# Two reorderings in the late attention steps of a four-layer conditioned sequence model, on one NeuronCore

## The chip, the cores and the metric

One NeuronCore of one Trainium2 chip runs the whole program. The metric is device time in microseconds (us) of one execution. The engines are TensorE (PE in the profile, its weight loads PEld), VectorE (DVE), ScalarE (ACT), GpSimd (POOL) and SyncE (SP, which only issues DMAs here). Each engine runs its own list of instructions in order, and waits on counting semaphores that other engines raise.

## The reference, cut to what matters

Four layers are applied to x of 64 sequences x 64 tokens x 256 features. The change touches the attention half of the second one (16 heads of 16 features, `split` makes the heads, `t` is the condition of a sequence):

```
def _rmsnorm(x):
    return x * jax.lax.rsqrt(jnp.mean(x * x, axis=-1, keepdims=True) + EPS)
...
def _ada_rmsnorm(x, t, gamma_w, beta_w):
    gamma = (t @ gamma_w.T)[:, None, :]
    beta = (t @ beta_w.T)[:, None, :]
    return gamma * _rmsnorm(x) + beta
...
q = split(x @ W_q.T)
k = split(x @ W_k.T)
v = split(x @ W_v.T)
attn = jax.nn.softmax(scale * jnp.einsum('bnqd,bnkd->bnqk', q, k), axis=-1)
o = jnp.einsum('bnqk,bnkd->bnqd', attn, v)
o = o.transpose(0, 2, 1, 3).reshape(b, l, dm)
return o @ W_o.T
...
x = x + a_alpha * _attention(_ada_rmsnorm(x, t, attn_gamma_w, attn_beta_w), W_q, W_k, W_v, W_o)
```

The first layer before it is a quantised gated MLP, the second half of the second layer is a SwiGLU MLP, the third is an adapter with weights made for each sequence, and the fourth is a layer norm with a conditional shift. All are computed in fp32 accuracy, with each matmul's operands split into a high and a low part (three products in place of one).

## The kernel before, in words

The kernel is written by hand for each engine. The program runs through four stages, one after the other and overlapped at their edges: the first layer up to about 224 us of the trace, attention up to about 383 us, the SwiGLU MLP up to about 690 us, adapter and norm to the end.

Attention works on 16 tiles of 256 tokens (4 sequences). It is a software pipeline of 17 steps, t = 0 to 16: the function `attention_body(s)` of each engine writes what that engine does in step t, for tiles of different age. `s.live(n)` means that tile t - n exists. Steps up to 8 are written out one by one ("peeled"), steps 9 to 14 are a hardware loop of two steps a turn, steps 15 and 16 are written out again. `plain(s)` is true for steps 9 to 16, `before_plain(s)` for 8 to 16. In a plain step t:

- TensorE, in this order: `scores` of tile t-2 (L1215), `transposes(s, 0)` of tile t-3 (L1237), `output` of tile t-4 (L1281), `transposes(s, 1)` of tile t-3, then `keys` and `queries` of tile t-1 (both L1156, 12 matmuls each, keys first), `weighted_values` of tile t-3 (L1254), `values` of tile t-1 (L1191).
- GpSimd: the attention input of tile t is made in four operations on 128x512 elements, in `attention_input`: part 0 multiplies x by its row scale (L182), part 1 multiplies by gamma (L186) and adds beta (L188), part 2 subtracts the high part to give the low part (L191). Between parts 1 and 2 it adds the attention output to x (`residual`, L1056). Behind part 2 it normalises the softmax of tile t-2 in two halves of 128x1024, `normalise(s, 0)` and `normalise(s, 1)` (both L1047). Part 0 for the next step's tile is issued at the end of the step, from step 8 on.
- ScalarE: `take_values` (L1465 to L1469), `take_transposed(s, 0)` (L1448), `exponentials(s, 0)` (L1440), `take_transposed(s, 1)`, `attention_input_high` of tile t (L198), which rounds the input to its high part, `exponentials(s, 1)`, `take_keys` of tile t-1 (L1476, two instructions), `take_queries` (L1485), `output_high` (L1491).
- VectorE: `maxima` of the two halves (L1643, L1647) with `scaled_output` between them (L1678), `sums` of the two halves (L1655, L1658), `output_low` (L1664).

What ties the engines together near the change: `transposes(s, 1)` in step t waits for `normalise(s, 1)` of step t-1 (semaphore `norm_done`). `take_keys` waits for the key matmuls (`k_ready`). `attention_input_high` waits for part 1 (`h_done`), and part 2 on GpSimd waits for `attention_input_high` (`h_hi_done`). `exponentials(s, 1)` stands ahead of `sums(s, 1)` on VectorE, whose reciprocal (L1658) `normalise(s, 1)` needs. Part 0 waits for part 2 of the tile before it, because both use the one buffer `mlp_in`. Tiles called `mlp_in`, `mlp_in_hi`, `mlp_in_lo`, `att_in_hi` and `att_in_lo` in L182 to L198 are that attention input.

After step 15 GpSimd makes the MLP's first input (L812, L816, L819), with the last normalisations and residuals between its parts, and TensorE goes over from attention to the MLP.

Of the kernel before, what the change touches and what calls it, by code (L numbers as in the profile page):

```python
# [92 lines left out]
def wait(eng, sem, count):  # L93

    if not isinstance(count, int) or count > 0:
        eng.wait_ge(sem, count)
# [72 lines left out]
def attention_input(nc, pool, core, s, part):  # L169

    x, cond, stat, h, S = core["x"], core["cond"], core["stat"], core["att_in"], core["att_sems"]
    t = s.at(0)
    hi, lo = (parts[s.slot(0, 2)] for parts in core["att_parts"])
    hb = h[:].rearrange("p h (b l) -> p h b l", b=GB1)

    def of_batches(v):
        return cond[:, v, :, bass.ds(t * GB1, GB1)].unsqueeze(3).to_broadcast([P, DH, GB1, L])

    if part == 0:
        pool.wait_ge(core["stat_loaded"], 16 * s.turn(0, 2))  # L180
        wait(pool, S["h_ready"], t)
        nc.gpsimd.tensor_tensor(h[:], x[:, :, bass.ds(t * GT1, GT1)], stat[:, bass.ds(t * GT1, GT1)].unsqueeze(1).to_broadcast([P, DH, GT1]),  # L182
                                ALU.mult).then_inc(S["xn_done"], 1)
    elif part == 1:
        pool.wait_ge(S["xn_done"], 2 * t + 1)
        nc.gpsimd.tensor_tensor(hb, hb, of_batches(GAMMA1), ALU.mult).then_inc(S["xn_done"], 1)  # L186
        pool.wait_ge(S["xn_done"], 2 * t + 2)
        nc.gpsimd.tensor_tensor(hb, hb, of_batches(BETA1), ALU.add).then_inc(S["h_done"], 1)  # L188
    else:
        pool.wait_ge(S["h_hi_done"], t + 1)  # L190
        nc.gpsimd.tensor_tensor(lo, h[:], hi.bitcast(FP32), ALU.subtract).then_inc(S["h_ready"], 1)  # L191


def attention_input_high(nc, act, core, t, k):

    S = core["att_sems"]
    act.wait_ge(S["h_done"], t + 1)
    nc.scalar.activation(core["att_parts"][0][k], core["att_in"][:], ACT.Copy).then_inc(S["h_hi_done"], 1)  # L198
# [633 lines left out]
def layers(nc, io, core, bank, keep, early, adapter_w, base_w, slot_loaded, out):  # L832
# [19 lines left out]
    with ExitStack() as c:  # L852
# [79 lines left out]
        def pair_of(ap, two):  # L932

            return ap[:, 2 * two:2 * two + 2, :].rearrange("p u k -> p (u k)")
# [5 lines left out]
        def plain(s):  # L940

            return not isinstance(s.t, int) or s.t > PEELED

        def before_plain(s):

            return not isinstance(s.t, int) or s.t >= PEELED
# [11 lines left out]
        def groups(ap):  # L958
            return ap.rearrange("p (a k) -> p a k", k=L)
# [81 lines left out]
        def _(pool):  # L1041
            def normalise(s, two):
                if s.live(2):
                    u = s.at(2) * PAIRS + two
                    pool.wait_ge(A["rec_done"], u + 1)
                    pu = groups(pair_of(p, two))
                    nc.gpsimd.tensor_tensor(pu, pu, rec[:, two, :].unsqueeze(2).to_broadcast([P, 16, L]),  # L1047
                                            ALU.mult).then_inc(A["norm_done"], 1)

            def residual(s):  # L1050
                if s.live(4):
                    t = s.at(4)
                    xt = x[:, :, bass.ds(t * GTA, GTA)]
                    pool.wait_ge(A["ya_done"], t + 1)
                    hold(pool, A["passed"])
                    nc.gpsimd.tensor_tensor(xt, xt, ya1[:], ALU.add).then_inc(A["x_done"], 1)  # L1056

            def attention_body(s):
                following = Step(s.t + 1, s.k + 1, NA, s.turns)
                if s.live(0):  # L1060
                    if not plain(s):
                        attention_input(nc, pool, core, s, 0)
                    attention_input(nc, pool, core, s, 1)
                    if s.first_tile(4):
                        first["row_scales"](pool, e35)
                    if plain(s):
                        residual(s)
                    if s.first_tile(3):
                        normalise(s, 0)
                    wait(pool, A["v_ready"], s.at(1) if s.live(2) else 0)  # L1070
                    attention_input(nc, pool, core, s, 2)
                    if not plain(s):
                        residual(s)
                if not s.first_tile(3):
                    normalise(s, 0)
                normalise(s, 1)
                if before_plain(s) and following.live(0):
                    attention_input(nc, pool, core, following, 0)

            def generator_base():  # L1080
                pool.wait_ge(A["base_loaded"], 32)
                nc.gpsimd.tensor_scalar(delta_bias, delta_bias, 0.1, None, ALU.mult).then_inc(A["base_done"], 1)
                pool.wait_ge(A["base_done"], 1)
                nc.gpsimd.tensor_tensor(base, base, delta_bias, ALU.add).then_inc(A["base_done"], 1)
# [350 lines left out]
        def _(act):  # L1435
            def exponentials(s, two):
                if s.live(2):
                    u = s.at(2) * PAIRS + two
                    act.wait_ge(A["sub_done"], u + 1)
                    nc.scalar.activation(pair_of(p, two), pair_of(p, two), ACT.Exp, scale=SCALE).then_inc(A["exp_done"], 1)  # L1440
# [20 lines left out]
            def take_values(s):  # L1461
                if s.live(2):
                    act.wait_ge(A["v_ready"], s.at(2) + 1)
                    wait(act, A["pv_ready"], s.at(3) if s.live(4) else 0)
                    nc.scalar.activation(value_slots(s, 0, 0), value_sums(s, 0, 0), ACT.Copy)  # L1465
                    nc.scalar.activation(value_slots(s, 0, 1), value_sums(s, 0, 1), ACT.Copy).then_inc(A["v_low_done"], 1)
                    if not vector_takes_values(s):
                        nc.scalar.activation(value_slots(s, 1, 0), value_sums(s, 1, 0), ACT.Copy)
                        nc.scalar.activation(value_slots(s, 1, 1), value_sums(s, 1, 1), ACT.Copy).then_inc(A["v_high_done"], 1)  # L1469

            def take_keys(s):
                if s.live(1):
                    act.wait_ge(A["k_ready"], s.at(1) + 1)
                    wait(act, A["s_ready"], UNITS * (s.at(1) - 1) if s.live(3) else 0)
                    for parity in range(2):
                        ins = nc.scalar.activation(ks[:, s.slot(1, 2)].rearrange("p c b e k -> p (c b) e k")[:, :, parity, :],  # L1476
                                                   bank[1].rearrange("p (a k) -> p a k", k=L), ACT.Copy,
                                                   scale=vecs[:, V_EVEN + parity:V_EVEN + parity + 1])
                    ins.then_inc(A["k_done"], 1)

            def take_queries(s):
                if s.live(1):
                    act.wait_ge(A["q_ready"], s.at(1) + 1)
                    ps = bank[5] if s.first_tile(1) else bank[2]
                    nc.scalar.activation(qs[:, s.slot(1, 2)], ps[:, :].rearrange("p (c t) -> p c t", c=2), ACT.Copy).then_inc(A["q_done"], 1)  # L1485
# [14 lines left out]
            def attention_body(s):  # L1500
                take_values(s)
                if s.first_tile(3):
                    first["square_rows"](act, e34)
                    first["take_x"](act, e35)
                if s.first_tile(3):
                    take_keys(s)
                take_transposed(s, 0)
                exponentials(s, 0)
                first_two = s.first_tile(3) or s.first_tile(4)
                take_transposed(s, 1)  # L1510
                if first_two:
                    exponentials(s, 1)
                if s.first_tile(3):
                    take_queries(s)
                if s.live(0):
                    wait(act, A["v_ready"], s.at(1) if s.live(2) else 0)
                    attention_input_high(nc, act, core, s.at(0), s.slot(0, 2))
                if not first_two:
                    exponentials(s, 1)
                if not s.first_tile(3):  # L1520
                    take_keys(s)
                    take_queries(s)
                output_high(s)
                if s.first_tile(4):
                    first["take_lines"](act, e37)
                rstd(s)
                square(s)
# [658 lines left out]
```

## Time and profile before

| | |
|---|---|
| median of 3 runs | 741.57 us (741.37 to 742.21) |
| the profiled execution | 741.11 us, of which the span of the trace is 739.3 us |
| PE busy, whole span | 721.8 us (98%) |
| PEld busy | 586.4 us (79%) |
| DVE busy | 514.7 us (70%) |
| POOL busy | 410.6 us (56%) |
| ACT busy | 359.3 us (49%) |
| granted TensorE clock, all 40 slices | 9 tenths or more |

A busy share is an average over the four stages. What the change is worth has to be read in the attention stage, from which instruction waits for which. PE's busy time there is modelled (matmuls overlap), so a PE row that looks unbroken can still hide a wait of a few tenths of a us.

### The profile page before, as it was taken

How to read it: one execution, taken by the hardware profiler on the slowest of the kernel's cores; microseconds unless marked ns; L12 is line 12 of the kernel's file. 1: busy time of each engine (PE TensorE's matmuls, PEld its weight loads, DVE VectorE, ACT ScalarE, POOL GpSimd, SP SyncE). 2: the span in 40 equal slices, each digit the busy share in tenths (PEclk: the TensorE clock that was granted, in tenths of full speed). 3: DMA queues.
4: the chain of work that ended last, by engine and by line, in shares of the span. 5: the costliest groups of instructions: out<-in, count | busy, mean ns of one | idle time of the engine just before them, and what ended most of it. 6: DMA issues, size and time to landing. Idle time of an engine off the chain costs nothing.

```text
span 739.3 us, 18704 instructions
## 1 busy us (share of the span) xinstructions
PE 721.8 (98%) x6700; PEld 586.4 (79%) x6700; DVE 514.7 (70%) x808; ACT 359.3 (49%) x722; POOL 410.6 (56%) x408
## 2 busy tenths in 40 slices
PE   9999999999999899999999999999999999999996
PEld 8888888888888788888888777777777767778884
DVE  4977777777789989888995465656655566453466
ACT  4534444344447677888874333333333332322585
POOL 5645655554678888999997624224242423320244
PEclk9999999999999999999999999999999999999999
DMA  8854544445432000000004255577667777759943
GB/s 301 258 111 99 108 121 101 100 111 121 110 73 63 22 28 17 17 1 0 1 4 134 104 173 175 177 220 216 191 190 251 212 215 231 238 160 390 386 178 142
DMA packets 81339, 106.25 MB, mean 144 GB/s; under 512 B 39904, under 2 KB 53376, under 8 KB 81152
## 3 DMA queue, kind: packets, MB, share of 16 engines
q1 hardware_dynamic: 79840, 103.34, 46.7%
q10 hardware_dynamic: 1440, 2.11, 1.1%
q8 instruction: 39, 0.64, 0.4%
q14 instruction: 20, 0.16, 0.1%
HBM read 75.77 MB, written 21.27 MB: 131 GB/s over the span
## 4 chain that ended last, share of the span: by engine, by line
PE 75%; POOL 16%; issue 5%; DVE 3%; ACT 1%; DMA 0%; POOLq 0%; DVEq 0%; SPq 0%; ACTq 0%
PE banks L446 24%; PE banks L1317 22%; PE banks L1347 12%; POOL p_sb L1047 5%; PE banks L1369 4%; PE banks L530 4%; POOL mlp_in L182 2%; PE banks L1979 2%; PE banks L1949 2%; POOL mlp_in L186 2%; POOL x_sb L1056 2%; POOL att_in_lo L191 1%; PE banks L1971 1%; POOL mlp_in L188 1%; PE banks L548 1%
## 5 line engine op out<-in xcount | busy, mean ns | idle before, releaser
L629 ACT ACTIVATE gelu<-banks,rstd 128x512 f32<-128x512 f32 x64 | 44.0, 688 | 115.8 <-PE banks L446 114.1
L1699 DVE TENSOR_TENSOR g<-banks,silu 128x512 f32<-128x512 f32 x64 | 44.2, 690 | 77.6 <-PE banks L1317 44.9
L1703 DVE TENSOR_TENSOR g_lo<-g,g_hi 128x512 fp32r<-128x512 f32 x64 | 55.7, 870 | 47.6 <-ACT g_hi L1539 47.6
L1539 ACT ACTIVATE g_hi<-g 128x512 fp32r<-128x512 f32 x64 | 40.4, 631 | 96.0 <-DVE g L1699 95.0
L1533 ACT ACTIVATE silu<-banks 128x512 f32<-128x512 f32 x64 | 38.2, 597 | 97.4 <-PE banks L1317 97.4
L446 PE MATMUL banks<-up_hi,xs_hi 128*128 128x512 f32 x254 | 81.1, 400 | 0.0
L446 PE MATMUL banks<-up_hi,xs_lo 128*128 128x512 f32 x256 | 79.2, 391 | 0.0
L1317 PE MATMUL banks<-mlp_in_hi,w_hi 128*128 128x512 f32 x252 | 78.8, 394 | 0.0
L446 PE MATMUL banks<-up_lo,xs_hi 128*128 128x512 f32 x256 | 78.8, 390 | 0.0
L1317 PE MATMUL banks<-mlp_in_lo,w_hi 128*128 128x512 f32 x252 | 78.0, 390 | 0.0
L1317 PE MATMUL banks<-mlp_in_hi,w_lo 128*128 128x512 f32 x252 | 77.8, 390 | 0.0
L745 DVE SCALAR_TENSOR_TENSOR h<-banks,rstd,gelu 128x512 f32<-128x512 f32 x64 | 47.8, 747 | 37.0 <-ACT gelu L629 37.0
L822 POOL TENSOR_TENSOR mlp_in_lo<-mlp_in,mlp_in_hi 128x1024 fp32r<-128x1024 f32 x8 | 19.9, 2490 | 80.7 <-ACT mlp_in_hi L829 80.7
L1047 POOL TENSOR_TENSOR p_sb<-p_sb,rec 128x1024 f32<-128x1024 f32 x32 | 60.4, 1906 | 5.2 <-DVE rec L1658 5.2
L446 PEld LDWEIGHTS banks<-up_hi,xs_lo 128*128 128x128 f32 x256 | 48.1, 188 | 10.4
L446 PEld LDWEIGHTS banks<-up_lo,xs_hi 128*128 128x128 f32 x256 | 48.1, 188 | 10.2
L1317 PEld LDWEIGHTS banks<-mlp_in_lo,w_hi 128*128 128x128 f32 x252 | 47.3, 188 | 10.7
L1317 PEld LDWEIGHTS banks<-mlp_in_hi,w_hi 128*128 128x128 f32 x252 | 47.2, 188 | 10.8
L1317 PEld LDWEIGHTS banks<-mlp_in_hi,w_lo 128*128 128x128 f32 x252 | 47.3, 188 | 10.2
L1347 PE MATMUL banks<-g_hi,w_hi 128*128 128x512 f32 x128 | 52.6, 411 | 0.7 <-DVE g_lo L1703 0.7
L446 PEld LDWEIGHTS banks<-up_hi,xs_hi 128*128 128x128 f32 x254 | 45.4, 188 | 8.3 <-issue 0.2
L1347 PE MATMUL banks<-g_hi,w_lo 128*128 128x512 f32 x128 | 50.6, 395 | 0.0
(230 smaller groups left out, 1736.2 us busy)
## 6 DMA issues: line engine op xcount, KB each, us to landing
gen_hyper<-in_gen_t SPq DMA_DIRECT2D x32, 512.0 KB, 4.4
gen_made<-base_w SPq DMA_DIRECT2D x64, 256.0 KB, 4.4
adapter_w<-gen_made SPq DMA_DIRECT2D x64, 256.0 KB, 4.4
tokens<-in_x_tok SPq DMA_DIRECT2D x32, 128.0 KB, 2.3
w_stage<-in_w_t SPq DMA_DIRECT2D x32, 128.0 KB, 2.6
tokens_again<-in_x_tok SPq DMA_DIRECT2D x32, 128.0 KB, 2.2
weight_slot<-adapter_w SPq DMA_DIRECT2D x4, 1024.0 KB, 8.8
x_sb<-in_x_t SPq DMA_DIRECT2D x7, 512.0 KB, 6.3
```

The costliest lines, as they stand in the source:

```text
L446: last = nc.tensor.matmul(up_bank(s, j, part)[:, :], (xs_hi, xs_lo)[a][:, k, d, :], up[b][:, d, at:at + 512], start=start and d == 0, stop ...
L530: last = nc.tensor.matmul(y_ps, qt[:, s.slot(2, 2), f, :], downq[:, f, :], start=f == 0, stop=f == FC - 1)
L629: nc.scalar.activation(gelu[:, j, :], up_bank(s, j, 1)[:, :], ACT.Gelu, scale=rstd0[:, bass.ds(s.at(0), 1)]).then_inc(Z["gelu_done"], 1)
L745: nc.vector.scalar_tensor_tensor(out=h[:, k, j * 512:(j + 1) * 512], in0=up_bank(s, j, 0)[:, :], scalar=rstd0[:, bass.ds(t, 1)], in1=gelu[ ...
L1047: nc.gpsimd.tensor_tensor(pu, pu, rec[:, two, :].unsqueeze(2).to_broadcast([P, 16, L]), ALU.mult).then_inc(A["norm_done"], 1)
L1317: last = nc.tensor.matmul(chunk_bank(s, f, i)[:, :], w1[a][:, at:at + P], hs[b][k][:, d, :], start=n == d == 0, stop=n == 2 and d == DH - 1)
L1347: last = nc.tensor.matmul(bank[5 + m][:, :], w1[a][:, at:at + P], gs[b][:, f % 2, :], start=f == n == 0, stop=f == FC - 1 and n == 2)
L1369: last = nc.tensor.matmul(ps[B * half:B * (half + 1), :], scaled[rows, :], hyper[rows, k, half, :], start=True, stop=True)
L1533: nc.scalar.activation(silu[:, f % 2, :], chunk_bank(s, f, 0)[:, :], ACT.Silu).then_inc(S["silu_done"], 1)
L1539: nc.scalar.activation(gs[0][:, f % 2, :], g[:, f % 2, :], ACT.Copy).then_inc(S["g_hi_done"], 1)
L1699: nc.vector.tensor_tensor(g[:, f % 2, :], chunk_bank(s, f, 1)[:, :], silu[:, f % 2, :], ALU.mult).then_inc(S["g_done"], 1)
L1703: nc.vector.tensor_tensor(gs[1][:, f % 2, :], g[:, f % 2, :], gs[0][:, f % 2, :].bitcast(FP32), ALU.subtract).then_inc(S["g_ready"], 1)
```

## The change

Two edits, each a change of order and nothing else. No instruction is added or removed, and no operand changes.

```diff
--- before.py
+++ after.py
@@ -1073,9 +1073,9 @@
                         residual(s)
                 if not s.first_tile(3):
                     normalise(s, 0)
-                normalise(s, 1)
                 if before_plain(s) and following.live(0):
                     attention_input(nc, pool, core, following, 0)
+                normalise(s, 1)
 
             def generator_base():
                 pool.wait_ge(A["base_loaded"], 32)
@@ -1512,13 +1512,16 @@
                     exponentials(s, 1)
                 if s.first_tile(3):
                     take_queries(s)
+                if plain(s):
+                    take_keys(s)
                 if s.live(0):
                     wait(act, A["v_ready"], s.at(1) if s.live(2) else 0)
                     attention_input_high(nc, act, core, s.at(0), s.slot(0, 2))
                 if not first_two:
                     exponentials(s, 1)
+                if not plain(s) and not s.first_tile(3):
+                    take_keys(s)
                 if not s.first_tile(3):
-                    take_keys(s)
                     take_queries(s)
                 output_high(s)
                 if s.first_tile(4):
```

GpSimd, end of step 8, the first of seven steps (8 to 14) in which this order changes. `mlp_in<-x_sb,stat` is part 0 of the next tile's input, `p_sb<-p_sb,rec` a half of the normalisation.

```order
 L191 TENSOR_TENSOR mlp_in_lo<-mlp_in,mlp_in_hi 128x512
 L1056 TENSOR_TENSOR x_sb<-x_sb,y_alpha 128x2x256
-L1047 TENSOR_TENSOR p_sb<-p_sb,rec 128x1024 x2
-L182 TENSOR_TENSOR mlp_in<-x_sb,stat 128x512
+L1047 TENSOR_TENSOR p_sb<-p_sb,rec 128x1024
+L182 TENSOR_TENSOR mlp_in<-x_sb,stat 128x512
+L1047 TENSOR_TENSOR p_sb<-p_sb,rec 128x1024
```

Part 0 of the next input now stands ahead of the second half of the normalisation, which comes later by that one operation.

ScalarE, step 15; steps 9 to 14 change in the same way, and step 16, which has no `att_in_hi`, has the keys ahead of the exponential. `k_sb` are the keys, `att_in_hi` the high part of the input, `p_sb<-p_sb` the exponential of the second half.

```order
 L1440 ACTIVATE p_sb<-p_sb 128x1024
 L1448 ACTIVATE pt_sb<-banks 128x1024
+L1476 ACTIVATE k_sb<-banks,vecs 128x8x64 x2
 L198 ACTIVATE att_in_hi<-mlp_in 128x512
 L1440 ACTIVATE p_sb<-p_sb 128x1024
-L1476 ACTIVATE k_sb<-banks,vecs 128x8x64 x2
 L1485 ACTIVATE q_sb<-banks 128x512
 L1491 ACTIVATE ot_hi<-banks 128x512
```

The two copies of the keys now stand ahead of the input's high part and of the second exponential. The orders of TensorE, VectorE and SyncE are the same before and after.

## Rows read from the trace of the kernel before

**Rows 1.** The page: the chain that ended last, shares of the span.
```profile
PE 75%; POOL 16%; issue 5%; DVE 3%; ACT 1%; DMA 0%; POOLq 0%; DVEq 0%; SPq 0%; ACTq 0%
```

**Rows 2.** Chain of waits, 318 to 362 us: its shares by line.
```profile
by line: POOL p_sb L1047 31.7%; issue 27.7%; POOL mlp_in L182 14.3%; POOL mlp_in L186 9.5%; POOL x_sb L1056 7.2%; POOL att_in_lo L191 3.4%; POOL mlp_in_lo L191 3.2%; POOLq L86 0.9%; POOL mlp_in L188 0.8%; POOLq L182 0.7%; POOLq L186 0.6%; P
```

**Rows 3.** Busy time (and records) per engine, first of seven steps, and all.
```profile
297.61:307.58 9.97, 9.44 (x206) 8.49 (x205) 8.03 (x9) 7.83 (x14) 9.57 (x9) 1.00 0.10 31
...
sum 69.49, PE 67.72 PEld 61.66 DVE 61.12 ACT 56.37 POOL 67.01; mean PE 9.67 PEld 8.81 DVE 8.73 ACT 8.05 POOL 9.57
```

**Rows 4.** Timeline, GpSimd, 347 to 359 us: start, duration, line, operation.
```profile
347.41 3.77 POOL L1047 TENSOR_TENSOR p_sb<-p_sb,rec 128x1024 f32<-128x1024 f32 x2
351.14 1.30 POOL L182 TENSOR_TENSOR mlp_in<-x_sb,stat 128x512 f32 x1
352.63 1.05 POOL L186 TENSOR_TENSOR mlp_in<-mlp_in,cond_vectors 128x512 f32<-128x512 f32 x1 [0.20 <-POOL mlp_in L182]
...
354.87 1.30 POOL L1056 TENSOR_TENSOR x_sb<-x_sb,y_alpha 128x512 f32 x1
356.12 1.30 POOL L191 TENSOR_TENSOR mlp_in_lo<-mlp_in,mlp_in_hi 128x512 fp32r<-128x512 f32 x1
357.37 1.92 POOL L1047 TENSOR_TENSOR p_sb<-p_sb,rec 128x1024 f32<-128x1024 f32 x1
```

**Rows 5.** Timeline, TensorE, 351 to 360 us.
```profile
351.91 0.72 PE L1237 MATMUL banks<-ident,p_sb 64*128 64x64 f32 x16
...
353.84 0.40 PE L1156 MATMUL banks<-att_in_hi,w_lo 128*128 128x256 f32 x2
...
355.58 1.10 PE L1254 MATMUL banks<-pt_sb,v_sb 128*32 128x64 f32 x64
...
358.26 1.20 PE L1215 MATMUL banks<-k_sb,q_sb 32*64 32x128 f32 x64
```

**Rows 6.** Timeline, ScalarE, 352 to 359 us.
```profile
353.37 1.00 ACT L1448 ACTIVATE pt_sb<-banks 128x1024 f32<-128x1024 f32 x1
354.94 0.63 ACT L198 ACTIVATE mlp_in_hi<-mlp_in 128x512 fp32r<-128x512 f32 x1 [0.57 <-POOL mlp_in L188]
355.48 1.04 ACT L1440 ACTIVATE p_sb<-p_sb 128x1024 f32<-128x1024 f32 x1
356.43 1.25 ACT L1476 ACTIVATE k_sb<-banks,vecs 128x512 f32<-128x512 f32 x2
357.56 0.60 ACT L1485 ACTIVATE q_sb<-banks 128x512 f32<-128x512 f32 x1
```

**Rows 7.** Timeline, GpSimd to TensorE, 380 to 384 us.
```profile
380.23 1.91 POOL L1047 TENSOR_TENSOR p_sb<-p_sb,rec 128x1024 f32<-128x1024 f32 x1
...
382.29 0.71 PE L1237 MATMUL banks<-ident,p_sb 64*128 64x64 f32 x16 [0.69 <-POOL p_sb L1047]
```

**Rows 8.** Timeline, TensorE to ScalarE, 339 to 342 us.
```profile
339.77 0.72 PE L1237 MATMUL banks<-ident,p_sb 64*128 64x64 f32 x16
...
340.61 1.02 ACT L1448 ACTIVATE pt_sb<-banks 128x1024 f32<-128x1024 f32 x1 [0.45 <-PE banks L1237]
```

**Rows 9.** Timeline, ScalarE to GpSimd, 262 to 265 us.
```profile
262.46 0.63 ACT L198 ACTIVATE att_in_hi<-mlp_in 128x512 fp32r<-128x512 f32 x1 [1.25 <-POOL mlp_in L188]
...
263.24 1.29 POOL L191 TENSOR_TENSOR att_in_lo<-mlp_in,att_in_hi 128x512 fp32r<-128x512 f32 x1 [0.87 <-ACT att_in_hi L198]
```

**Rows 10.** Timeline, VectorE, 349 to 359 us.
```profile
349.89 1.23 DVE L1643 TENSOR_REDUCE mx<-banks 128x16 f32<-128x1024 f32 x1 [0.47 <-PE banks L1215]
...
356.52 0.25 DVE L1658 RECIPROCAL rec<-rsum 128x16 f32<-128x16 f32 x1
356.69 1.16 DVE L1655 TENSOR_REDUCE rsum<-p_sb 128x16 f32<-128x1024 f32 x1
357.89 0.25 DVE L1658 RECIPROCAL rec<-rsum 128x16 f32<-128x16 f32 x1
```

**Rows 11.** Busy time per engine, then granted clock (1.00 is full), 256 to 298 us.
```profile
256.00:298.00 42.00, 39.16 (x832) 35.73 (x832) 37.20 (x45) 32.20 (x54) 37.89 (x29) 1.00 0.09 29
```


## The prediction

> **What bounds the kernel now.** I read the page first. Its chain that ended last is 75% TensorE and 16% GpSimd [rows 1], so somewhere GpSimd sets the pace. The chain of waits cut to 318 to 362 us, the late attention steps, says where: nearly all of it lies on GpSimd, with the normalisation L1047 at 31.7% and the four input operations and the residual behind it; TensorE does not show at the head of it [rows 2]. The table by stretches confirms it. From the first normalisation of step 8 to that of step 15 are 69.49 us in seven steps, 9.93 us each, of which GpSimd is busy 67.01 [rows 3]. TensorE shows 67.72 there, but its ends are modelled, so the row hides small waits.
>
> Then the timelines, each from one step's first normalisation, which I call 0 (347.41). GpSimd: the first half starts at 0, the second at 1.87 (half of 351.14 - 347.41), part 0 of the next input (L182) at 3.73, L186 at 5.22 after a gap of 0.20, L1056 at 7.46, L191 at 8.71, and the next first half at 9.96 [rows 4]. There is no idle time but the gaps in which L186 and L188 wait for their own predecessor. This is a closed ring on one engine. TensorE, same zero: second transposes at 4.50, the twelve key matmuls end at 6.83 (353.84 + 0.40), weighted values at 8.17, scores at 10.85 [rows 5]. ScalarE: it ends the copy of the second transposes at 6.96, stands idle 0.57 until L188 is done, makes the input's high part from 7.53 to 8.16, the exponential at 8.07, the keys at 9.02, the queries at 10.15 [rows 6].
>
> **GpSimd's edit.** Part 0 goes between the two halves. Two things follow. It takes away a gap: L186 today starts 1.49 after L182 (352.63 - 351.14), while two operations of that size without a dependence stand 1.25 apart (356.12 - 354.87) [rows 4]; with 1.9 us of normalisation between them the wait is over long before. That is 0.24 a step. And it moves the end of the second half: it ended at 1.87 + 1.91 = 3.78, and now ends at 1.87 + 1.25 + 1.91 = 5.03. TensorE's second transposes wait for that. Today they start at 4.50 because the output matmuls ahead of them last that long. From the end of a normalisation to the transposes that wait for it are 0.15 us (380.23 + 1.91 = 382.14, then 382.29) [rows 7], so they now start at 5.18, 0.68 later. All behind them on TensorE's list comes as much later: keys, queries, weighted values, values.
>
> **ScalarE's edit.** The keys go ahead of the input's high part. Taken alone this fills the idle 0.57: the copy of the transposes ends at 6.96, the keys are there at 6.83, the copies take 1.13 (357.56 - 356.43), the high part 0.63 [rows 6], and it ends at 8.72 in place of 8.16. GpSimd's L191, which needs it, stands at 8.71. So alone it would cost GpSimd about nothing, at most 0.1 a step.
>
> **The two together.** Now L191 depends on the key matmuls, and these on the second half of the normalisation. The new ring, with each term:
>
> - 0 to 5.03: first half, part 0, second half [rows 4, 7]
> - 5.18: transposes start, + 0.15 [rows 7]
> - 7.51: last key matmul ends, + 2.33 (354.24 - 351.91) [rows 5]
> - 7.63: ScalarE starts on the keys, + 0.12, as from the end of transposes to their copy (339.77 + 0.72 = 340.49, then 340.61) [rows 8]
> - 8.76: the high part starts, + 1.13; 9.39: it ends, + 0.63 [rows 6]
> - 9.44: L191 starts. In the written-out steps 0.15 lie between (262.46 + 0.63 = 263.09, then 263.24) [rows 9]. In the loop I have no case of it waiting. The bounds are nothing and 0.15, and I take 0.05: GpSimd stands at L191 for nothing else by then.
> - 10.69: the next first half, + 1.25 (357.37 - 356.12) [rows 4].
>
> A step is then 10.69 against 9.93, 0.76 more. The residual L1056 ends at about 8.5 and GpSimd stands still for some 0.9. The order of GpSimd changes in steps 8 to 14 and that of ScalarE in 9 to 16, so the ring closes seven times, at L191 of steps 9 to 15: 7 x 0.76 = 5.3 us.
>
> What is read from the Trainium skill beside this: "Advanced Engine Details and Errata", under Miscellaneous Facts, puts reading a semaphore from a sequencer at 50 to 100 ns. By that figure the three handoffs would be 0.15 to 0.30 in place of my 0.32, the step 10.52 to 10.67, and the loss 4.1 to 5.2 us, an estimate from that page; my first handoff row, 0.15, is above it.
>
> **What does not become late.** The second exponential goes to 9.30, starts 1.2 later than today in the step and ends at 10.34. VectorE's second sum and reciprocal take 1.45 from there (358.14 - 356.69) [rows 10], to 11.8; the second half that needs it starts at 10.69 + 3.12 = 13.8. The queries end at about 10.85, the scores start at about 11.0, and from VectorE's first maximum to its first reciprocal are 6.88 (356.77 - 349.89) [rows 10]: done at 11.0 + 1.3 (the scores' 1.20 and a handoff) + 6.9 = 19.2, where the normalisation of two steps on needs it at 21.4. The slack is 2 us. The moved instructions issue no DMA, and SyncE's list is the same.
>
> **Whether the loss reaches the end.** At the edge of attention TensorE waits 0.69 us for GpSimd's last second half (382.29) [rows 7], so what GpSimd is late there, TensorE is late. From there on TensorE is the chain, and it gives nothing back. In step 15 the following tile does not exist and the halves stand together, as before, so step 16's transposes are not held. I count the full 5.3. The profiled execution took 741.11 and the median is 741.57, so the sum is 746.4 on the profiled one and 746.8 on the median, which I forecast.
>
> **The rivals.**
>
> - *A faster kernel.* Only the gap goes: 7 x 0.24 = 1.7 us less, 739.9. For it: the whole ring on GpSimd is shorter by that, and ScalarE's idle time is filled. Against it: L191 would have to find the high part done at 9.93 - 0.24 - 1.25 = 8.44, so the keys would have to start at 8.44 - 0.05 - 0.63 - 1.13 = 6.63; they can't before 7.63. It decides itself there: the key matmuls would have to end 1 us sooner than I have them. 5%.
> - *Nothing to be seen.* The two edits meet otherwise than I think (the transposes are held for less, or part of the exit gives it back), and the stall is about as large as the gap won: 741.6, within 1.5. 4%.
> - *More than that.* Each handoff costs 0.15 or more and the copies of the keys 1.25 in full rather than 1.13: step 10.69 + 0.13 + 0.12 = 10.94, loss 7.1, 748.7, and beyond it if a further wait closes. 4%.
> - *The clock.* TensorE would be idle 10.69 - 9.67 = 1.0 us of each step [rows 3]. In the written-out steps, 256 to 298 us, it is busy 39.16 of 42 and the granted clock is 1.00, the 2.4 GHz level [rows 11]; 9.67 of 10.69 is hardly less. There is no row at 1.2 GHz here. Were all of seven steps at that level, their 9.67 of work would be 19.3, and the loss 66 us. 1%. The Trainium skill ("TensorE: Matmul & The Clock Gate", Part 1) has the clock halved behind an idle array; the row of the written-out steps goes against that here.
>
> **How the numbers follow.** The forecast has 86%. Its bounds: with no time at all for the three handoffs the step is 10.69 - 0.32 = 10.37 and the loss 7 x 0.44 = 3.1, 744.7; with 0.15 for each it is 10.82 and 6.2, 747.8, and with the keys in full, 748.7, of which I take in most: 748.4. The range 744.7 to 748.4 holds nearly all of the 86%, and leaves out the faster, the equal and the extreme cases. A measurement of this kernel can tell 0.2%, 1.5 us, from no change. Faster by more: the first rival, 5%. Within: the second, 4%. Slower by more: the rest, 91%.
>
> **What the profile after would show.** Right: in steps 9 to 15 GpSimd idle 0.8 to 1.0 before L191, released by ScalarE's L198; first halves 10.6 to 10.8 apart; TensorE's second transposes 0.1 to 0.2 behind the end of the second half, with some 0.6 idle ahead; ScalarE idle before the keys (L1476) and not before L198; L186 right behind the second half with no gap. The stretch from 297.6 us to TensorE's transposes now at 382.29 longer by 5, and all behind it of the same length. Wrong: L191 starting with no wait, or ScalarE's keys starting straight behind the copy of the transposes. I would be wrong above all if the key matmuls were not held by the second transposes, or if the exit had slack that I don't see.

## The result, and the profile after

The changed kernel takes 747.07 us (median of 5 runs, 746.31 to 747.77), beside 742.14 of 5 runs of the kernel before (741.37 to 742.21). The two medians are 4.93 us apart. The ratio on record is 1.0073, 95% interval 1.0062 to 1.0085, which on 742 us is 4.6 to 6.3 us lost. The two profiled spans, 739.3 and 744.8 us, differ by 5.5. One of the ten executions of E3 below took 797.81 us at a granted clock of 0.85, where all others have 0.995 or more: its median counts that one (741.38 without it), its ratio does not.

First the page of the kernel after: the chain that ended last, its shares of the span.

```profile
PE 74%; POOL 12%; issue 8%; DVE 4%; ACT 1%; DMA 0%; POOLq 0%; DVEq 0%; SPq 0%; ACTq 0%
```

Beside [rows 1], GpSimd's share fell from 16% to 12% and "issue" rose from 5% to 8%. Read alone, this would say that GpSimd matters less now. The chain of waits for 318 to 362 us, shares by line, looks the same way at first.

```profile
by line: issue 53.9%; POOL x_sb L1056 11.8%; POOL mlp_in L182 11.6%; POOL mlp_in L186 9.6%; POOL mlp_in_lo L191 8.8%; POOL p_sb L1047 1.7%; POOL mlp_in L188 0.8%; POOLq L1045 0.8%; POOL att_in_lo L191 0.8%; POOLq L86 0.7%; POOLq L182 0.7%; 
```

In [rows 2] the normalisation L1047 had 31.7% and "issue" 27.7%; now L1047 has 1.7% and "issue" 53.9%. The pieces of the same view, from 350 to 362 us, are all GpSimd's. Three of them (start, length, what):

```profile
351.18 0.90 issue
...
359.35 0.92 issue
...
360.31 1.29 POOL mlp_in_lo L191
```

The first lies inside the first half, which runs from 350.86: the view has put most of the normalisation's own time under "issue", which is one trap here. The second is real idle time ahead of L191, and the view does not name the engine that ends it, which is the other. Both have to be read from timelines. In those of the kernel after, lines behind ScalarE's edit are three higher (VectorE's L1658 is now L1661).

Next the busy time (and records) per engine, from one step's first normalisation half to the next one's: the first of the seven steps, the last, and all.

```profile
297.39:308.10 10.71, 9.77 (x209) 8.78 (x208) 7.90 (x9) 8.62 (x15) 9.55 (x8) 1.00 0.08 28
...
361.56:372.25 10.69, 9.80 (x210) 8.92 (x210) 8.93 (x11) 8.40 (x15) 9.54 (x8) 1.00 0.01 2
sum 74.86, PE 68.72 PEld 62.40 DVE 61.10 ACT 58.73 POOL 66.84; mean PE 9.82 PEld 8.91 DVE 8.73 ACT 8.39 POOL 9.55
```

Seven steps take 74.86 in place of 69.49 [rows 3], 10.69 each in place of 9.93, and that is 5.37 of the 5.5 us. GpSimd's busy time has not grown (66.84 beside 67.01), so the difference is idle time. TensorE's row grew from 67.72 to 68.72 with the same matmuls, so it isn't good to better than 1 us in these steps. Here is one step on GpSimd: start, duration, line, operation, and in brackets the idle time ahead and who ended it.

```profile
350.86 1.90 POOL L1047 TENSOR_TENSOR p_sb<-p_sb,rec 128x1024 f32<-128x1024 f32 x1
352.73 1.27 POOL L182 TENSOR_TENSOR mlp_in<-x_sb,stat 128x512 f32 x1
353.95 1.90 POOL L1047 TENSOR_TENSOR p_sb<-p_sb,rec 128x1024 f32<-128x1024 f32 x1
355.81 1.04 POOL L186 TENSOR_TENSOR mlp_in<-mlp_in,cond_vectors 128x512 f32<-128x512 f32 x1
357.04 1.04 POOL L188 TENSOR_TENSOR mlp_in<-mlp_in,cond_vectors 128x512 f32<-128x512 f32 x1 [0.19 <-POOL mlp_in L186]
358.05 1.31 POOL L1056 TENSOR_TENSOR x_sb<-x_sb,y_alpha 128x512 f32 x1
360.31 1.29 POOL L191 TENSOR_TENSOR mlp_in_lo<-mlp_in,mlp_in_hi 128x512 fp32r<-128x512 f32 x1 [0.95 <-ACT mlp_in_hi L198]
361.56 1.90 POOL L1047 TENSOR_TENSOR p_sb<-p_sb,rec 128x1024 f32<-128x1024 f32 x1
```

One reads down the starts. The first half, part 0 and the second half follow each other, and L186 starts with no idle time in its row, where it had 0.20 [rows 4]. Then L191 stands 0.95 for ScalarE's high part. In the seven steps this wait is 0.97, 0.91, 0.97, 0.96, 0.98, 0.95 and 1.07; the last is step 15, which is written out. The same step on TensorE: first transposes, second transposes, the last pair of the twelve key matmuls, weighted values, scores.

```profile
352.91 0.71 PE L1237 MATMUL banks<-ident,p_sb 64*128 64x64 f32 x16
...
356.00 0.71 PE L1237 MATMUL banks<-ident,p_sb 64*128 64x64 f32 x16 [0.79 <-POOL p_sb L1047]
...
357.93 0.40 PE L1156 MATMUL banks<-att_in_hi,w_lo 128*128 128x256 f32 x2
...
359.67 1.10 PE L1254 MATMUL banks<-pt_sb,v_sb 128*32 128x64 f32 x64
...
362.28 1.21 PE L1215 MATMUL banks<-k_sb,q_sb 32*64 32x128 f32 x64
```

The second transposes, which had no wait in [rows 5], stand 0.79 for GpSimd's second half. On ScalarE, same step:

```profile
356.75 1.03 ACT L1448 ACTIVATE pt_sb<-banks 128x1024 f32<-128x1024 f32 x1 [0.19 <-PE banks L1237]
358.45 1.27 ACT L1476 ACTIVATE k_sb<-banks,vecs 128x512 f32<-128x512 f32 x2 [0.67 <-PE banks L1156]
359.60 0.63 ACT L198 ACTIVATE mlp_in_hi<-mlp_in 128x512 fp32r<-128x512 f32 x1
360.12 1.05 ACT L1440 ACTIVATE p_sb<-p_sb 128x1024 f32<-128x1024 f32 x1
361.07 0.60 ACT L1485 ACTIVATE q_sb<-banks 128x512 f32<-128x512 f32 x1
```

The 0.57 ahead of L198 in [rows 6] is gone, and 0.67 ahead of the keys (L1476) has come, because ScalarE now stands at the keys before TensorE has made them. L198 starts as soon as ScalarE is free. The whole stretch, 297.6 to 372 us, by who waits for whom (total us, times, longest):

```profile
DVE rsum L1658 <- ACT p_sb L1440: 8.6, 7, 1.4
...
PE banks L1237 <- POOL p_sb L1047: 5.1, 8, 0.8
...
ACT k_sb L1476 <- PE banks L1156: 4.6, 7, 0.7
...
POOL att_in_lo L191 <- ACT att_in_hi L198: 4.0, 4, 1.1
...
POOL mlp_in_lo L191 <- ACT mlp_in_hi L198: 2.8, 3, 1.0
```

Three of these lines close a circle: TensorE's L1237 waits for GpSimd, ScalarE's L1476 for TensorE, GpSimd's L191 for ScalarE, each in every step. VectorE's 8.6 is the longest total and is outside the circle, as the slack worked out below shows. Last, the edge to the MLP, beside [rows 7]:

```profile
385.38 1.93 POOL L1047 TENSOR_TENSOR p_sb<-p_sb,rec 128x1024 f32<-128x1024 f32 x1
...
387.45 0.71 PE L1237 MATMUL banks<-ident,p_sb 64*128 64x64 f32 x16 [0.78 <-POOL p_sb L1047]
```

TensorE's last second transposes were at 382.29 and are at 387.45, 5.16 later. Step 8 started 0.22 earlier in this execution (297.39 beside 297.61), so together that is the 5.37 of the steps: the way from 372.25 to the edge gives nothing back.

### The profile page after: what moved, and what is told of

Same layout as the page of the kernel before. It is cut to its first block, busy times and chain, and to the rows that moved or that the text cites. A ratio compares the mean times of both kernels' runs of the same rounds, so it can differ in the third digit from the quotient of the medians.

```text
span 744.8 us, 18704 instructions
## 1 busy us (share of the span) xinstructions
PE 722.3 (97%) x6700; PEld 586.7 (79%) x6700; DVE 514.4 (69%) x808; ACT 361.5 (49%) x722; POOL 411.9 (55%) x408
## 4 chain that ended last, share of the span: by engine, by line
PE 74%; POOL 12%; issue 8%; DVE 4%; ACT 1%; DMA 0%; POOLq 0%; DVEq 0%; SPq 0%; ACTq 0%
PE banks L446 24%; PE banks L1317 22%; PE banks L1347 12%; PE banks L1369 4%; PE banks L530 4%; POOL p_sb L1047 3%; PE banks L1982 2%; POOL mlp_in L182 2%; PE banks L1952 2%; POOL x_sb L1056 2%; POOL mlp_in L186 1%; DVE mx L1646 1%; PE banks L1974 1%; PE banks L548 1%; POOL mlp_in_lo L191 1%
## 5 line engine op out<-in xcount | busy, mean ns | idle before, releaser
L1047 POOL TENSOR_TENSOR p_sb<-p_sb,rec 128x1024 f32<-128x1024 f32 x32 | 60.7, 1905 | 5.1 <-DVE rec L1661 5.1
```

## The experiments

Each kernel was timed against the kernel before on the same chip. E1 to E4 share one set of its runs (median 741.68), E5 to E8 another (741.70), E9 and E10 a third (741.37). Distances are between the first normalisation halves of steps 8 to 15, read from the profiled execution of each kernel; in the kernel before they are 9.97, 9.95, 9.94, 10.00, 9.94, 9.96 and 9.73.

### E1 and E2: each edit alone

```diff
E1, GpSimd's edit on the kernel before:
-                normalise(s, 1)
                 if before_plain(s) and following.live(0):
                     attention_input(nc, pool, core, following, 0)
+                normalise(s, 1)
E2, ScalarE's edit on the kernel before:
+                if plain(s):
+                    take_keys(s)
                 if s.live(0):
...
-                if not s.first_tile(3):
+                if not plain(s) and not s.first_tile(3):
                     take_keys(s)
+                if not s.first_tile(3):
                     take_queries(s)
```

> GpSimd's edit alone: part 0 of the next input between the halves, ScalarE as before. Theory (the loss is a ring that needs both edits): the high part still follows L188 at once, L191 never waits for more than 0.1 us, the second transposes still wait 0.6 to 0.8 us for the second half. The step is then set either by GpSimd at 9.7 us or by the way over TensorE's values and scores and VectorE back to the first half, which from rows of before I put at about 9.87. First halves 9.7 to 9.95 apart, 740.5 to 742.3 us. Rival A (the late second half is the loss by itself, since TensorE is held each step): 0.7 us more a step, 746.5 to 747.5. Rival B (only the gap goes): 9.69 a step, 740.4.

Measured: 742.17 us, ratio 1.0016 (1.0004 to 1.0028). The distances are 9.69, 10.11, 9.88, 9.92, 10.00, 9.89, 9.74, sum 69.23, beside 69.49. Chain of waits for 318 to 362 us by line, and two rows of GpSimd:

```profile
by line: PE banks L1156 27.6%; PE banks L1281 18.2%; PE banks L1191 16.4%; PE banks L1237 13.9%; PE banks L1215 13.3%; PE banks L1254 9.4%; issue 1.5%
```

```profile
345.66 1.30 POOL L191 TENSOR_TENSOR att_in_lo<-mlp_in,att_in_hi 128x512 fp32r<-128x512 f32 x1
347.21 1.91 POOL L1047 TENSOR_TENSOR p_sb<-p_sb,rec 128x1024 f32<-128x1024 f32 x1 [0.25 <-DVE rec L1658]
```

L191 does not wait, so with the keys in their old place there is no ring. But the gap of 0.24 is not won either: only the first distance, 9.69 in place of 9.97, is shorter by about that much. Afterwards the chain is TensorE's list alone, with no GpSimd line in it, and GpSimd's first half waits a little for VectorE's reciprocal. TensorE's own list of some 9.9 us stands right behind GpSimd's. One expectation missed. I had the second transposes wait 0.6 to 0.8 for the second half in each step, and they wait once, 0.4. In the other steps they start as late behind the first half as in the changed kernel (352.36 - 347.21 = 5.15), but TensorE's own list brings it there no sooner. The ratio a little over 1 has no cause on record. The seven steps are 0.26 shorter and the span is 0.4 longer, so in the profiled execution the loss is outside the steps. The last two pairs of halves, behind step 15, stand 10.89 apart in place of 10.20, but in E3 they stand 10.62 apart and its ratio is 1.0002.

> ScalarE's edit alone: keys ahead of the high part, GpSimd as before. Theory: the key matmuls end at 6.8 us behind the first half, the high part at 8.7 and L191 starts on its turn or up to 0.1 us late: first halves 9.93 to 10.05 apart, 741.5 to 742.8 us. Rival A (the keys ahead of the high part are the loss by themselves): 746.5 to 747.5. Rival C (the second exponential later on ScalarE is the loss, through VectorE's second sum): it would show here too, above 744.

Measured: 741.66 us, ratio 1.0002 (0.9992 to 1.0011). Distances 10.24, 9.95, 9.98, 9.93, 9.96, 9.94, 9.87, sum 69.87. L191 waits once, 0.23 in step 9, and then no more. ScalarE's wait for the key matmuls stands in the waits, but from step 10 on L191 does not wait behind it:

```profile
ACT k_sb L1476 <- PE banks L1156: 2.0, 7, 0.5
```

The 0.38 over the sum of the kernel before is mostly the first step. So neither edit costs the 5 us. They cost it together.

### E3: both edits, but the keys behind the high part

```diff
-                if plain(s):
-                    take_keys(s)
                 if s.live(0):
                     wait(act, A["v_ready"], s.at(1) if s.live(2) else 0)
                     attention_input_high(nc, act, core, s.at(0), s.slot(0, 2))
+                if plain(s):
+                    take_keys(s)
                 if not first_two:
                     exponentials(s, 1)
```

> Both edits, but the keys one place later on ScalarE: high part, keys, second exponential. Only the place of the high part differs from the changed kernel. Theory (ring through the high part): L191 does not wait, the loss is gone, first halves 9.8 to 10.0 apart, 740.8 to 742.5 us. Rival C (the keys ahead of the second exponential delay the sum, its reciprocal and the low part of the output): the loss stays in full or in most, 744.5 to 747.

Measured: 741.43 us, ratio 1.0002 (0.9992 to 1.0012); distances 9.69, 10.10, 9.81, 9.99, 9.91, 9.88, 9.75, sum 69.13, and L191 waits in none of them. The keys still stand ahead of the second exponential, so it is their place ahead of the high part, and that alone, which costs.

### E4: the full change in every other step

```diff
-                if plain(s):
+                if plain(s) and s.slot(0, 2):
                     take_keys(s)
...
-                if not plain(s) and not s.first_tile(3):
+                if not (plain(s) and s.slot(0, 2)) and not s.first_tile(3):
                     take_keys(s)
```

GpSimd keeps its new order in all steps; ScalarE has its new one in steps 9, 11, 13 and 15.

> Both edits, but ScalarE's only in steps 9, 11, 13 and 15; GpSimd's in all. Theory: four steps of about 10.7 us and, between them, three of about 9.7 (in which the time lost has caught TensorE up, so that GpSimd alone sets the step), in turn: 4 x 0.76 - 3 x 0.24 = 2.3 us over the kernel before, 743.9 to 744.9. Rival (a delay that builds up from step to step, or one that a single occurrence starts off for all later steps): no alternation in the distances between first halves, and 746 or more.

Measured: 744.42 us, ratio 1.0042 (1.0026 to 1.0059); distances 10.71, 9.69, 10.89, 9.71, 10.89, 9.72, 10.72, sum 72.33. The loss comes step by step where both orders meet. The short steps are 9.69 to 9.72, which E1 had only once: as I read it, behind a long step TensorE has time in hand, and GpSimd's shorter list can be used. The 10.89, 0.2 over the 10.70 of the full change, is the other side of that. Rows of such a step, whose first half is at 317.96: the second transposes, and L191.

```profile
323.28 0.71 PE L1237 MATMUL banks<-ident,p_sb 64*128 64x64 f32 x16
```

```profile
327.60 1.30 POOL L191 TENSOR_TENSOR att_in_lo<-mlp_in,att_in_hi 128x512 fp32r<-128x512 f32 x1 [1.15 <-ACT att_in_hi L198]
```

The transposes come 5.32 after the first half, without a wait, in place of 5.14: TensorE, behind a step of 9.69, is itself that much late, and the ring takes it over. The total fell in the expected range, 743.9 to 744.9, though the seven steps lost 2.84 (72.33 - 69.49) and not 2.3.

### E5 and E6: the keys later on TensorE, with and without the change

```diff
-                keys(s)
+                if not plain(s):
+                    keys(s)
                 queries(s)
+                if plain(s):
+                    keys(s)
                 weighted_values(s)
```

E5 has this on top of the change, E6 on the kernel before. Lines behind it are three higher again (in E5 the keys are L1479).

> The changed kernel with TensorE's twelve query matmuls ahead of the twelve key matmuls in steps 9 to 16. Same work, keys done 1.5 us later in the step. Theory (the key matmuls are a link of the ring): the ring is longer by just these 1.5 us, first halves 12.1 to 12.3 apart, 7 x 1.5 = 10.5 us over the changed kernel, 756.5 to 758.5. Rival (the keys are not in it, the loss comes from the late exponential or transposes): within 1 us of the changed kernel, 746.5 to 748.

Measured: 757.11 us, ratio 1.0201 (1.0185 to 1.0216); distances 12.12, 12.10, 12.12, 12.10, 12.10, 12.12, 12.09, sum 84.75. One step from its first half at 346.47: TensorE's second transposes and last key matmuls, ScalarE's keys and high part, GpSimd's L191 and next first half.

```profile
351.61 0.71 PE L1237 MATMUL banks<-ident,p_sb 64*128 64x64 f32 x16 [0.78 <-POOL p_sb L1047]
...
354.96 0.39 PE L1156 MATMUL banks<-mlp_in_hi,w_lo 128*128 128x256 f32 x2
```

```profile
355.48 1.27 ACT L1479 ACTIVATE k_sb<-banks,vecs 128x512 f32<-128x512 f32 x2 [2.09 <-PE banks L1156]
356.63 0.63 ACT L198 ACTIVATE att_in_hi<-mlp_in 128x512 fp32r<-128x512 f32 x1
```

```profile
357.34 1.27 POOL L191 TENSOR_TENSOR att_in_lo<-mlp_in,att_in_hi 128x512 fp32r<-128x512 f32 x1 [2.40 <-ACT att_in_hi L198]
358.57 1.90 POOL L1047 TENSOR_TENSOR p_sb<-p_sb,rec 128x1024 f32<-128x1024 f32 x1
```

Every term but one is that of the change. The last key matmul ends at 8.88 (354.96 + 0.39 - 346.47) in place of 7.47, 1.41 later, and the step is 12.11 in place of 10.69, 1.42 longer. What delays the keys comes back in full in each step.

> The same swap of queries and keys in the kernel before. Theory: there the keys end 0.7 us ahead of even the swapped time that ScalarE needs them at (8.35 after the first half, copies at 9.02), and nothing that waits for them is in the ring of GpSimd: no difference, 741 to 742.5 us, first halves 9.93 apart. Rival (TensorE's order is a cost of its own): over 744 here too.

Measured: 741.84 us, ratio 0.9997 (0.9988 to 1.0007); distances 9.97, 9.94, 9.98, 9.94, 9.96, 9.96, 9.72, sum 69.47, as before to 0.02. The same delay of the keys costs nothing where the keys don't stand in the ring. The rival that TensorE's order is a cost of its own falls with this. How long TensorE's list is, a swap does not test.

### E7: the ring opened on GpSimd's side

```diff
-                    if s.first_tile(3):
+                    if s.first_tile(3) or plain(s):
                         normalise(s, 0)
                     wait(pool, A["v_ready"], s.at(1) if s.live(2) else 0)
...
-                if not s.first_tile(3):
-                    normalise(s, 0)
-                if before_plain(s) and following.live(0):
-                    attention_input(nc, pool, core, following, 0)
+                if not plain(s):
+                    if not s.first_tile(3):
+                        normalise(s, 0)
+                    if before_plain(s):
+                        attention_input(nc, pool, core, following, 0)
                 normalise(s, 1)
+                if plain(s) and following.live(0):
+                    attention_input(nc, pool, core, following, 0)
```

ScalarE keeps the keys ahead of the high part. On GpSimd part 2, L191, now stands between the two halves, and part 0 behind the second.

> ScalarE as in the changed kernel; on GpSimd in steps 9 to 15 the low part (L191) stands between the two halves in place of part 0 of the next input, which goes behind the second half again. The second half is as late behind the first as in the changed kernel, and TensorE is held as there, but the first half no longer waits for the high part. Theory: the ring has one normalisation and a part 0 more of slack and does not close: first halves 9.9 to 10.0 apart in steps 10 to 15, 741 to 743 us. Rival (the late second half and late keys cost by themselves): 745 or more.

Measured: 742.98 us, ratio 1.0013 (1.0003 to 1.0022); distances 9.56, 10.23, 9.91, 9.92, 10.00, 9.93, 9.73, sum 69.28. GpSimd in one of the steady steps, and the first half of step 9:

```profile
307.93 1.91 POOL L1047 TENSOR_TENSOR p_sb<-p_sb,rec 128x1024 f32<-128x1024 f32 x1 [1.06 <-DVE rec L1664]
```

```profile
337.99 1.92 POOL L1047 TENSOR_TENSOR p_sb<-p_sb,rec 128x1024 f32<-128x1024 f32 x1
339.85 1.29 POOL L191 TENSOR_TENSOR mlp_in_lo<-mlp_in,mlp_in_hi 128x512 fp32r<-128x512 f32 x1
341.08 1.92 POOL L1047 TENSOR_TENSOR p_sb<-p_sb,rec 128x1024 f32<-128x1024 f32 x1
342.94 1.30 POOL L182 TENSOR_TENSOR mlp_in<-x_sb,stat 128x512 f32 x1
```

ScalarE in the same step, the keys (L1479) and the high part:

```profile
345.60 1.27 ACT L1479 ACTIVATE k_sb<-banks,vecs 128x512 f32<-128x512 f32 x2 [0.27 <-PE banks L1159]
346.76 0.63 ACT L198 ACTIVATE att_in_hi<-mlp_in 128x512 fp32r<-128x512 f32 x1
```

They start 7.61 and 8.77 behind the first half at 337.99, as late as in the changed kernel (7.59 and 8.74). The lateness is all there and costs nothing, since the next first half no longer waits behind it. The wait at L191 is gone and the steps are back at 9.9 to 10.0. Part of the expectation missed: the second transposes start 5.16 behind the first half (343.15 - 337.99), as expected, but in most steps TensorE does not stand waiting for them, as in E1. The 1 us that is left (interval 0.2 to 1.6) is outside the seven steps in the profiled execution: from step 15's first half to the next one are 11.28 in place of 10.03, because the L191 that was spared in step 9 (where the first half comes up early, and stands 1.06 for its reciprocal) is paid there.

### E8 to E10: does a better version come of it?

The written-out steps, 10.6 us each, show L191 waiting 0.87 for the high part [rows 9], as the changed steps do now. If that wait were what sets their length, the order of the late steps should help there. E8 moves the residual and the scaled output early from step 5 on. E9 and E10 give all of the late order of the kernel before to steps 6 to 8 and 5 to 8.

```diff
E8:
-                    if plain(s):
+                    if plain(s) or s.t >= 5:
                         residual(s)
...
E9 (E10 has 4 for 5):
-    PEELED = 8
+    PEELED, LATE = 8, 5
...
-            return not isinstance(s.t, int) or s.t > PEELED
+            return not isinstance(s.t, int) or s.t > LATE
...
```

Not shown are the other halves of the same conditions, VectorE's scaled output in E8, and in E9 and E10 `before_plain` and a wait of TensorE whose count depended on `plain`.

> The kernel before, with the residual ahead of the low part in steps 5 to 8 too, and VectorE's scaled output ahead of its second maximum there. In these steps GpSimd stands 0.87 us before L191 for the high part; the residual of 1.25 us would fill it, as in steps 9 to 15. Theory: the step goes from 10.63 to 9.9 or 10.0 in four steps, less 0.7 each at most: 739 to 740 us. Rival (something else, TensorE or VectorE, sets 10.6 there): 741.5 to 742.

> The kernel before with all of the late steps' arrangement (values in their own bank, ScalarE taking all four value copies, residual and part 0 early) from step 6 on instead of step 9. In e8 the residual alone gave steps of 9.71 and 10.25 and then 10.6 again, with VectorE's reciprocal waited for and TensorE's values held by ScalarE's key copies, since values and keys share a bank there. Theory (the shared bank sets 10.6 in steps 5 to 8): three more steps of 9.95 instead of 10.63, 2.0 us less, 739.2 to 740.6. Rival (ScalarE, which has the early squares and value copies in these steps, becomes the bound): 741 to 743.

> The same from step 5 on: by the theory of e9 four more steps at 9.95, 2.7 us less than the kernel before, 738.6 to 740. By its rival no faster than e9, or slower, 741 to 743.

Measured: E8 741.25 us, ratio 0.9994 (0.9985 to 1.0003); E9 741.61, 1.0003 (0.9994 to 1.0012); E10 741.83, 1.0004 (0.9995 to 1.0013). My forecast of a gain missed in all three. In E8 the first of the steps falls to 9.71, and the next ones are 10.25, 10.58, 10.62 and 10.90, the last in place of 9.97: the wait moves from L191 to the first half. In E9 the same distances are 10.62, 9.75, 10.63, 10.79 and 10.60. Its waits on TensorE and GpSimd, 255 to 298 us:

```profile
PE banks L1281 <- ACT v_sb L1469: 1.8, 3, 0.6
POOL p_sb L1047 <- DVE rec L1658: 1.8, 2, 0.9
```

There GpSimd waits for VectorE's reciprocal, and TensorE's output matmuls for ScalarE's copies of the values. Shortening GpSimd's part in these steps gives the time to those two. The theory of the shared bank fell: E9 gives the values their own bank, and three of its steps are as long as before (10.60 to 10.79). Which of the two waits is the bound, and how they hang together, was not taken apart. None of the kernels is measurably faster than the kernel before.

## Why the prediction was right

**The sign and the mechanism.** The forecast was a closed ring GpSimd, TensorE, ScalarE, GpSimd, in seven steps, that exists only with both edits. The profile shows its three waits, E1 and E2 show that neither edit alone makes it, and E3, E5 and E7 move one link each with the effect that the ring asks for.

**The terms.** From the first half at 350.86, beside what the prediction has:

| | predicted | measured |
|---|---|---|
| second half ends | 5.03 | 4.99 (353.95 + 1.90) |
| second transposes start | 5.18 | 5.14 |
| last key matmul ends | 7.51 | 7.47 (357.93 + 0.40) |
| keys start on ScalarE | 7.63 | 7.59 |
| high part starts, ends | 8.76, 9.39 | 8.74, 9.37 |
| L191 starts | 9.44 | 9.45 |
| next first half | 10.69 | 10.70 |

The one unknown was the last handoff, bounded by nothing and 0.15 and taken at 0.05. It is 0.08 (360.31 - 360.23), 0.03 more, and the copies of the keys took 0.02 more; the second half ended 0.04 sooner than summed, which cancels most of both. Seven steps: 5.3 predicted, 5.37 measured.

**How near the total is.** 747.07 measured beside 746.8 forecast is nearer than the forecast deserves. It was counted on 741.57, the median of three runs, and that of five is 742.14. By the two medians the loss is 4.93 and not 5.3; beside the later medians of the kernel before, 741.68, 741.70 and 741.37, it is 5.4 to 5.7. The size rests on the distances in the trace, not on the total.

**By the page's figure.** The Trainium skill ("Advanced Engine Details and Errata", Miscellaneous Facts) gives 50 to 100 ns for reading a semaphore from a sequencer, which made the step 10.52 to 10.67 by the estimate in the prediction. The three handoffs here are 0.15, 0.12 and 0.08, 0.35 together, and the step is 10.69: just above the top of that range. The rows of this case were the better source; a handoff, from one operation's end to the other's start, may hold more than the reading.

**The full carry to the end.** Right at the edge, where it was argued (5.16 later, and 0.22 of earlier start). At the very end of the trace the shift is 5.5. The 0.3 between them arises in the MLP stage: the first of its matmuls L1369 starts 5.2 later than before (422.4 beside 417.2), the last 5.5 later (658.4 beside 652.9). The forecast had everything behind the edge of the same length. Executions of the kernel before differ by more (741.37 to 742.21), and I have no cause for it.

**TensorE's wait.** I had some 0.6 idle ahead of the second transposes, and it is 0.38 in step 9 and 0.72 to 0.79 in steps 10 to 15. The output matmuls ahead of them end sooner behind the first half, at 4.36 (354.83 + 0.39 - 350.86) and not at the 4.50 that I left standing. The ring's path goes through GpSimd there, so the length of the step does not change.

**The slack of VectorE.** The second reciprocal ends at 11.85 in the step (predicted 11.8), and the half that needs it starts at 13.79:

```profile
359.62 0.25 DVE L1661 RECIPROCAL rec<-rsum 128x16 f32<-128x16 f32 x1
361.21 1.22 DVE L1658 TENSOR_REDUCE rsum<-p_sb 128x16 f32<-128x1024 f32 x1 [1.34 <-ACT p_sb L1440]
362.46 0.25 DVE L1661 RECIPROCAL rec<-rsum 128x16 f32<-128x16 f32 x1
```

So the 1.34 that VectorE waits ahead of its sum is hidden, and the largest line of the waits is harmless. One number was loose. I let the scores start at 11.0, right behind the copied queries, and they start at 11.42 (362.28 - 350.86), because they stand behind TensorE's own values matmuls, which the delay of the transposes carries along. The first reciprocal, for scores started at 351.64, ends at 359.87 and is needed at 361.56: 1.7 of slack and not the 2.2 that the working gives (21.4 - 19.2). It changed nothing.

**The rivals.** *A faster kernel*: it put the point of decision at key matmuls 1 us sooner, and they are 0.04 sooner. Its price was wrong as well. E1 and E3, which have GpSimd's gain and no ring, save 0.26 and 0.36 in seven steps and not 1.7, since TensorE's list is the next bound at once; the prediction did not price that list. *Nothing to be seen*: E2 is what it would have looked like. *More than that*: the keys took 1.15 (359.60 - 358.45), not 1.25, and the handoffs stayed below 0.15 on average. *The clock*: TensorE is busy 68.72 of 74.86 in the seven steps and the granted clock is 1.00 in each of them, the 2.4 GHz level. The rule of the Trainium skill cited for it ("TensorE: Matmul & The Clock Gate", Part 1) halves the clock behind an idle array; waits of up to 0.8 us in each step did not bring that about here. In E5 TensorE waits up to 1.05 us at a time and is busy 69.95 of 84.75, and the granted clock is 1.00 there too. The prediction read the written-out steps as speaking against it here. TensorE is busy 39.16 of 42 in them, so they are no test of the rule itself, and no trace of this case shows it at work in these steps.

## What to carry to other kernels

When an operation is moved on one in-order engine, write the next step's start as a sum of terms through every engine that it reaches, and see whether the path comes back to where it started: two moves that each cost next to nothing (ratios 1.0016 and 1.0002) can close such a ring, and then each step pays the whole excess of it. Put the work whose result the next engine waits for ahead of work that waits itself (here the high part ahead of the keys). And before counting a gap on the busiest engine as gain, look at how far behind the next engine's own list is: here only 0.04 of the 0.24 us a step could be won (69.23 of seven steps in E1 beside 69.49).

## What the runs showed of the hardware

Two GpSimd operations of which the second reads the first's result stand further apart in the hardware loop than in the written-out steps. Two rows of a written-out step of the kernel after:

```profile
258.63 1.29 POOL L182 TENSOR_TENSOR mlp_in<-x_sb,stat 128x512 f32<-128x512 f32 x1
259.99 1.04 POOL L186 TENSOR_TENSOR mlp_in<-mlp_in,cond_vectors 128x512 f32<-128x512 f32 x1
```

Here L186 starts 0.07 behind the end of L182 (258.63 + 1.29 = 259.92). In the loop before it started 0.19 behind it (351.14 + 1.30 = 352.44, then 352.63 [rows 4]), and L188 behind L186 still does (355.81 + 1.04 = 356.85, then 357.04). That is 0.12 more a pair, and it isn't in the durations. The handoff from ScalarE to GpSimd differs the other way: 0.15 in the written-out steps [rows 9], 0.08 in the loop, in the change and in E5 alike. Step 15, written out again behind the loop, goes with the written-out steps in both: 0.09 from the end of L186 to L188 (366.51 + 1.04 = 367.55, then 367.64), and 0.15 from ScalarE to GpSimd (370.23 + 0.63 = 370.86, then 371.01). So both differences go with the loop. No run here says why.
